# Squares kept in PSUM, over their own input, instead of in a ring in SBUF

## The reference

```python
def _L0_rec_ref(embeds, inner_w):
    B, F, E, UNITS = (1024, 39, 64, 128)
    delta = jnp.einsum('uf,bfe->bue', inner_w, embeds)
    lp = jnp.sum(delta * delta, axis=-1)
    return lp
e = jnp.stack([tbl_0[ids[:, 0]], ..., tbl_38[ids[:, 38]]], axis=1)   # (2048, 39, 64)
z = _L0_rec_ref(e, L0_rec_inner_w)                                   # (2048, 128)
h = jnp.concatenate([z, dense_ctx], axis=1)
h = jnp.maximum(h @ W_top1 + b_top1, 0.0)
h = jnp.maximum(h @ W_top2 + b_top2, 0.0)
y = h @ W_top3                                                       # (2048, 1)
```

## Time and profile before

| what | value |
|---|---|
| median of 3 runs | 570.38 us (564.09 to 572.16) |
| the profiled execution's own time | 569.8 us |
| its span, first to last instruction | 568.1 us |
| mean granted TensorE clock | 0.916 of full speed |
| busy: PE / DVE / ACT / POOL | 445.9 / 440.6 / 224.3 / 412.0 us |

### The profile page before, as it was taken

The page is one execution under the profiler, slowest core; times in us unless marked ns, Lnnn a source line. Parts: engine busy times, 40 slices in busy tenths (PEclk is TensorE's granted clock), DMA queues, the critical chain, the costliest instruction groups (busy, mean ns, idle before and its releaser), DMA issues.

```text
span 568.1 us, 10177 instructions
## 1 busy us (share of the span) xinstructions
PE 445.9 (78%) x3376; PEld 388.9 (68%) x3376; DVE 440.6 (78%) x716; ACT 224.3 (39%) x312; POOL 412.0 (73%) x343
## 2 busy tenths in 40 slices
PE   0556869887799769968999879967998799865566
PEld 0556858786688659857878668856987698744334
DVE  2899759898689967868988967868989998854631
ACT  2543124243244433423533433443544444443432
POOL 6888778778777778778887878778887887872000
PEclk9997999899899888988999889988999999966677
DMA  6773477667776666748776666747766886474510
GB/s 174 211 198 88 116 213 228 201 176 191 187 210 191 192 165 172 212 111 222 207 197 188 192 177 177 211 123 223 213 203 171 227 218 187 129 214 123 183 50 1
DMA packets 67594, 100.43 MB, mean 177 GB/s; under 512 B 15750, under 2 KB 22554, under 8 KB 67548
## 3 DMA queue, kind: packets, MB, share of 16 engines
q1 hardware_dynamic: 56696, 88.61, 52.1%
q0 software_dynamic: 10752, 11.03, 10.3%
q10 hardware_dynamic: 100, 0.16, 0.1%
HBM read 36.31 MB, written 0.16 MB: 64 GB/s over the span
## 4 chain that ended last, share of the span: by engine, by line
POOL 72%; issue 19%; PE 4%; DMA 2%; SPq 1%; ACT 1%; DVE 1%; POOLq 0%; ACTq 0%
POOL x_all L389 72%; PE side L456 2%; PE side L448 1%; SPq L338 1%; PE delta L489 1%; DMA xs<-xl 1%; ACT sq_all L557 1%; DMA x_all<-tbl,idx 0%; DMA dense_f<-dense_t 0%; PE side L461 0%; PE turned L475 0%; DVE z L668 0%; DMA idx<-ids 0%; SPq L347 0%; ACT h L566 0%
## 5 line engine op out<-in xcount | busy, mean ns | idle before, releaser
L389 POOL DMA_INDIRECT x_all<-tbl,idx x336 | 411.3, 1224 | 103.6 <-issue 101.8
L431 PE MATMUL side<-table,onehot 125*128 125x192 bf16 x2496 | 245.2, 259 | 43.8 <-DVE table L718 19.1
L431 PEld LDWEIGHTS side<-table,onehot 125*128 125x128 bf16 x2496 | 218.1, 104 | 68.7 <-issue 48.8
L489 PE MATMUL delta<-xs,ws 117*128 117x512 f32 (+1 forms) x272 | 121.8, 488 | 63.2 <-DMA xs<-xl 48.5
L664 DVE TENSOR_TENSOR acc_all<-acc_all,sq_all 128x1024 f32<-128x1024 f32 x112 | 136.5, 1219 | 18.3 <-ACT sq_all L557 17.3
L541 ACT ACTIVATE xh<-turned 117x512 fp32r<-117x512 f32 x96 | 54.0, 562 | 208.4 <-PE turned L475 201.2
L637 DVE TENSOR_SCALAR onehot<-idh,row_no 125x1024 bf16<-125x1024 f16 x312 | 130.1, 481 | 6.9 <-DMA idh<-ids 6.9
L656 DVE TENSOR_REDUCE x_all<-side 128x128 f32<-128x384 f32 x144 | 77.0, 551 | 64.2 <-PE side L431 63.2
L557 ACT ACTIVATE sq_all<-delta 128x1024 f32<-128x1024 f32 x112 | 112.4, 1022 | 28.9 <-PE delta L489 27.9
L489 PEld LDWEIGHTS delta<-xs,ws 117*128 117x128 f32 x272 | 52.4, 211 | 82.6 <-DMA xs<-xl 41.5
L475 PEld LDWEIGHTS turned<-ident,x_all 128*117 128x117 f32 x352 | 86.3, 310 | 9.3 <-DMA x_all<-tbl,idx 6.1
(11 more groups left out here) (30 smaller groups left out, 80.5 us busy)
## 6 DMA issues: line engine op xcount, KB each, us to landing
xs<-xh SPq DMA_DIRECT2D x160, 234.0 KB
xs<-xl SPq DMA_DIRECT2D x80, 234.0 KB
idh<-ids SPq DMA_DIRECT2D x72, 224.0 KB
x_all<-tbl,idx POOLq DMA_INDIRECT x336
xs<-xh SPq DMA_DIRECT2D x32, 117.0 KB
x_all<-tbl SPq DMA_DIRECT2D x12, 224.0 KB
idh<-ids SPq DMA_DIRECT2D x72, 26.0 KB
xs<-xl SPq DMA_DIRECT2D x16, 117.0 KB
```

Source lines behind the costliest of these rows:

```text
L389: pool.indirect_dma_start(x_slots[k][:, f, 0:E], None, tables[f], bass.IndirectOffsetOnAxis(idx[k][:, f:f + 1], 0),).then_inc(gathered[k], 16)
L431: mm = pe.matmul(side[n % 2][:, q * PARTS * E:(q + 1) * PARTS * E], onehot[k % OHR][:, c, q, h * TB:(h + 1) * TB], table[k][:, q, c, :, :] ...
L489: mm = pe.matmul(delta[quad % 2][:, c:c + cols], ws[:, :], xs[i % XS][:, j, 0:SIZE[u], :].rearrange("p g b -> p (g b)"), start=True, stop= ...
```

## The change

The squares of quads 1 to 7 are written by ACT over their own input, in `delta0` or `delta1`. DVE's add takes its second operand from there. The ring `sq_all` in SBUF is gone, and the ids which used its memory at the very start use `acc_all` instead. ACT no longer waits for adds. PE, which overwrites `delta`, now waits for DVE's add of the quad two before (`summed`) where it waited for the square of it (`squared`); for quad 2 it still waits for the square of quad 0, which goes to `acc` as before. No instruction of an engine changes its place.

```diff
-SQ = 2
...
-        sq_all = sb("sq_all", [P, SQ, 4 * NB], F32)
-        sq = [sq_all[:, k, :] for k in range(SQ)]
-        ids_all = sq_all[0:PAIRS * STEPS, 0, 0:2 * NB].bitcast(I32)
-        ids_low = sq_all[0:PAIRS * STEPS, 1, 0:DUP * NB].bitcast(F16).rearrange("p (d c) -> p d c", d=DUP)
         acc_all = sb("acc_all", [P, 2, 4 * NB], F32)
+        ids_all = acc_all[0:PAIRS * STEPS, 0, 0:2 * NB].bitcast(I32)
+        ids_low = acc_all[0:PAIRS * STEPS, 1, 0:DUP * NB].bitcast(F16).rearrange("p (d c) -> p d c", d=DUP)
...
                     quad = n // 2
-                    if n % 2 == 0:
-                        wait(pe, squared, at_quads(s, h) + quad - 1)
+                    if n % 2 == 0 and quad == 2:
+                        pe.wait_ge(squared, at_quads(s, h) + 1)
+                    elif n % 2 == 0:
+                        wait(pe, summed, at_sums(s, h) + quad - (2 if quad > 2 else 1))
...
                 def square(s, h, quad):
                     act.wait_ge(projected, at_quads(s, h) + quad + 1)
-                    if quad == 0:
-
-                        to = acc[h]
-                    else:
-                        wait(act, summed, at_sums(s, h) + quad - 1 - (SQ - 1))
-                        to = sq[(h * (QUADS - 1) + quad - 1) % SQ]
+                    to = acc[h] if quad == 0 else delta[quad % 2]
                     act.activation(to[:, :], delta[quad % 2][:, :], ACT.Square).then_inc(squared, 1)
...
-                    dve.tensor_tensor(acc[h][:, :], acc[h][:, :], sq[(h * (QUADS - 1) + quad - 1) % SQ][:, :], ALU.add).then_inc(summed, 1)
+                    dve.tensor_tensor(acc[h][:, :], acc[h][:, :], delta[quad % 2][:, :], ALU.add).then_inc(summed, 1)
```

## The result

The changed kernel takes 579.52 us (median of 4 runs, 579.08 to 585.0), the kernel before 568.92 (median of 4, one run more than was known ahead). The ratio over the runs is 1.0213, 95% interval 1.0129 to 1.0297: slower, clear of no change, and at the edge of what 2% tells apart. The time lies 4.5 us over the forecast of 575; the medians are 10.6 us apart, nearly twice the 5.6 us that the forecast adds to its own starting point. The profiled execution is the longest of the four, 585.0; it lies 5.5 us over the median, which has to be kept in mind with its rows.

A forecast was written before the change was run, and what follows sets the result against it. The prediction took POOL, its gathers held by DVE's adds, to pace PE in steps 0 to 4 and at the end, with PE and DVE near full below it. 569.8 - 22.7 + 24.5 + 3.8 = 575.4, so 575 us; 8-in-10 range 557 to 593.

The forecast's parts named there:

- Part 1: POOL's gathers are no longer held by DVE's adds, 51.6 us off POOL; gain on the path 22.7 us.
- three terms: PE's idle times behind idx loads 12.9 us, PE's clock 4 us, PE's idling for the last gather 5.7 us.
- Part 2: PE's first projection of a quad waits for the add, not the square: 24.5 us in steps 0-6, 3.8 in the last.
- the waits cost more: Rival: every PE wait for adds is met in full, +37 us, with clock loss; 593 us, chance 0.22.
- The places: PE waits per step: odd quad 3 1.25 us, odd quad 5 0.2, odd quad 7 0.65, even quad 5 1.4.
- The sum: Whole kernel: 569.8 - 22.7 + 24.5 + 3.8 = 575.4 us; two large terms of opposite sign nearly cancel.
- POOL isn't freed: Rival: adds still hold POOL's gathers, so only PE's new waits act; about 590 us, chance 0.05.
- in-place squares are slow: Rival: ACT squares reading and writing one bank take up to 1.9 us, +18 us; 593 us, chance 0.05.
- POOL's freedom wins: Rival: PE's waits are mostly swallowed (17 us) and the whole 30 us comes back; 557 us, chance 0.18.
- steps over 62 us in 5 and 6: Sign of being wrong: steps 5 and 6 over 62 us would mean DVE's queue costs more than counted.

The follow-up runs named there:

- Late loads: Kernel before with IDX_AT 4.5 instead of 1.5, so the idx loads come later in SyncE's queue; 570.25 us, ratio 1.0049.
- one operand: Kernel before with the add replaced by an equally long VectorE instruction with a single SBUF input, summing of squares left out; 546.17 us against 569.98.
- the mix with six: Kernel before, but only quads 3, 5 of even and 1, 2, 3, 5 of odd sides use the SBUF ring, others squared in place; 545.68 us.
- the ring in odd sides alone: Kernel before, but only quads 1, 2, 3, 5 of odd sides use the SBUF ring; all even-side quads are in place; 559.93 us.
- wait-only kernel: Kernel before with only PE's wait changed to that of the changed kernel, squares still in the SBUF ring; 582.1 us, ratio 1.0218.

## Why the prediction was right, and where it was off

**What bounds the kernel: right.** POOL's rate set the end. Late loads left it where it was, one operand less took it away. That SyncE's queue is where PE feels POOL was right for the kernel before, but it is a place, not a cause.

**Part 1: right, also in size.** Forecast -22.7 us with bounds of 18.6 and 30; alone it measures -23.8. (The three terms of the forecast add up to 22.6, not 22.7.) POOL's last gather was forecast to end at 465 to 470 and ends at 469.5, which is partly luck: POOL's busy time fell by 57.5 us instead of 51.6, and 11.6 us of new waits for PE put the end back. The Trainium skill's page "SBUF — State Buffer", section "Who interferes with whom", has a rule that fits the adds: two SBUF inputs contend with a GpSimd instruction that reads SBUF, and at most one doesn't, outside of the two-port modes, a condition that the prediction left out. Three instructions with at most one SBUF input (subtraction, new add, one-element reduce) leave a gather at 0.94 us. One-hot rows, made from the SBUF tile `idh` and a column of `row_no`, do hold it; whether by a second input or by such a mode, no run here tells. The section's remark that `tensor_tensor` doesn't hold up descriptor generation doesn't fit: about 90 gathers of the kernel before were held by it. These gathers read their row numbers from SBUF, which would be why; that was not tried apart.

**Part 2: right in kind, too small, and with a term missing.** Forecast +24.5 + 3.8 = 28.3 us; beside the kernel with free gathers it measures 33.3. The experiments divide it in two. From the mix with six (545.7) to the ring in odd sides alone (559.9) quads 3 and 5 of even sides go in place: 14.3 us, where the prediction has 11.1. From there to the changed kernel (579.5) quads 1, 2, 3 and 5 of odd sides do: 19.6 us, where it has 7 x 2.1 + 1.15 = 15.9. So both are short by 3 to 4 us; with runs of one kernel 4 to 6 us apart, which by more is not settled.

What the prediction had at nothing is that PE also runs slower. The kernel with one operand, whose page follows, and its last step from the first transpose on, then the last step of the changed kernel in two stretches:

```profile
PE 441.3 (81%) x3376; PEld 385.7 (71%) x3376; DVE 442.1 (81%) x716; ACT 224.2 (41%) x312; POOL 357.5 (66%) x343
...
477.20:544.40 67.20, 44.42 (x148) 32.66 (x147) 34.06 (x34) 30.71 (x46) 0.00 (x0) 0.72 0.37 119
```
```profile
506.50:528.10 21.60, 13.89 (x46) 10.72 (x46) 13.41 (x15) 11.62 (x16) 0.00 (x0) 0.70 0.53 167
528.10:583.30 55.20, 34.80 (x103) 24.81 (x101) 21.05 (x20) 19.01 (x30) 0.00 (x0) 0.65 0.25 80
```

The two profiled spans, 583.3 and 544.4 us, are 38.9 apart (5.5 of it is the long execution). PE is busy 455.8 us against 441.3 for the same 3376 matmuls, 14.5 us more, at a mean granted clock of 0.909 against 0.927; its idle time grows by 24.4. Of its busy time 87 us fell into stretches at the half clock (1.2 GHz), against 65; if they took twice as long there, the clock makes some 11 of the 14.5 us (an estimate). The wait-only kernel, whose profiled execution is at its median, has 456.4 us busy as well. So idle time alone stayed under the 28.3 us forecast, and the rest is work that takes longer. The prediction counts the clock as a gain in part 1 (4 us); as a cost of the waits only the rival "the waits cost more" has it, 0.5 to 1 us a step. The last step takes 76.8 us against 67.2, +9.6 where 3.8 was forecast, and 4.3 of it is busy time.

The places were mostly right. Quad 3 of odd sides idles longest: 1.08 us in steps 4 to 6, but 1.85 to 3.94 in steps 0 to 3. There the square itself is late, because ACT's list has the rounding of `dense` just before it, which waits for its load: 6.4 us in step 0, 2.9 to 4.0 in steps 1 to 3 (with one operand 2.3 to 2.6). In all ACT waits 26.6 us for this load in the changed kernel, 22.7 before and 17.8 with one operand. The same can be seen in the last step of the kernel before, where PE stops at this place for the square:

```profile
534.57 0.42 ACT L547 ACTIVATE dense<-dense_f 128x256 fp32r<-128x256 f32 x1 [6.37 <-DMA dense_f<-dense_t]
534.90 1.01 ACT L557 ACTIVATE sq_all<-delta 128x1024 f32<-128x1024 f32 x1
...
536.05 1.19 PE L489 MATMUL delta<-xs,ws 117*128 117x512 f32 x2 [2.92 <-ACT sq_all L557]
```

So a part of what the rows put down to the add is a wait for `dense`, and of the 4.31 us in the last step of the changed kernel 2.92 were there before. Whether `dense` later in ACT's list would give it back was not tried.

At even sides the prediction passed over quads 1, 3, 4 and 7 (overlaps of 0.02 to 0.06 us at quads 4 and 7 in the trace of before). In the changed kernel they do start right at the end of the add, quads 4 and 7 in every step, quad 1 in six and quad 3 in four, but in steps 0 to 6 that adds only 0.1 to 0.9 us each. In the last step quads 4 and 5 of the even side were missed: their adds ended 1.2 and 1.5 us after PE's start in the trace of before, under cover of the 5.66 us for the last gather, which part 1 takes away.

**The sum.** -23.8 + 33.3 = +9.5 on 570, against the forecast +5.6 on 569.8. That the large terms nearly cancel was right, and with it that the sign hung on their difference. Its own range, 563 to 586, isn't worked out in it: with both terms at their bounds the sum reaches from 557 to 588.

**The rivals.** "POOL isn't freed" and "in-place squares are slow" are refuted by the rows of the changed kernel. "POOL's freedom wins" describes what the mix with six does, not the change. "The waits cost more" was half true: the waits cost 33.3 us of the 37 that it named, part of it by way of the clock, as it had it; but its steps over 62 us in 5 and 6 did not come (60.0 and 59.5), and the stops for `xs` did swallow part. The 65 ns more for each add from PSUM, the estimate from the Trainium skill's page "VectorE: DVE Perf Modes", section on the TRN2 errata, don't show: the add takes 1.210 us with one operand in PSUM against 1.217 before.

## What to carry to other kernels

A buffer that is written in place is held until its last reader is done. List, for each use, who wants it back and when. A use with less than about a microsecond to spare may become a wait, since the queues shift once one wait is added; what it costs is the time for which the engine then idles, and that went from 0.1 to 4.3 us here. Allow for a lower clock too: PE's longer busy time was about a third of the loss in the profiles. And when a wait is longer than its own chain (square and add, 1.3 us after PE is ready), look at what made the first link late; here it was a load in ScalarE's list. A resource that is freed and a wait that is added needn't go together: here eight of fourteen quads could give the gathers air and were hardly waited for (3.8 us), and that version beats both kernels (545.7 us against 568.5 and 579.5). Before moving work in a full engine's list, ask what stands behind it: earlier adds only made VectorE wait for squares.

## What the runs showed of the hardware

- A gather's descriptor writing (0.94 us) that starts during an add with both operands in SBUF mostly ends 0.81 to 0.97 us after that add (kernel before). With one operand in PSUM (changed kernel), or as a `tensor_reduce` of one element, VectorE's instruction doesn't hold it: 0.94 us in the median. One-hot rows (`tensor_scalar`, fp16 to bf16 in SBUF) hold it, 1.19 us in the median. VectorE's add doesn't get longer in any case (1.217, 1.210 and 1.209 us).
- ScalarE squaring 128x1024 floats from PSUM over its own input takes 1.016 us, as to SBUF (1.02).
- With more idle time PE was granted less clock: 0.909 in the mean and 455.8 us busy in the changed kernel, 0.927 and 441.3 us with one operand, for the same 3376 matmuls.
- Freeing the gathers saves 23.8 us beside PE's old waits and 2.6 beside its new ones; the new waits cost 33.3 us beside freed gathers and 12.1 beside held ones.
